# Third attention of an eight-block kernel: expert rows added, and statistics of x taken, in other tiles of the batch loop

## The chip, the cores and the metric

The kernel runs on one core of one Trainium2 chip. The metric is the device time of one execution in microseconds (us). The engines are TensorE (PE, with its weight loads as PEld), VectorE (DVE), ScalarE (ACT), GpSimd (POOL) and SyncE (SP, which issues transfers here).

## The reference

A residual stream x of 8 batches by 512 tokens by 256 features goes through four pairs of a cross attention and a feed-forward block. Each block is applied to the layer norm of x and added to x:

```
x = x + L0_xcond(layernorm(x), ctx, ...);  x = x + L0_ffn(layernorm(x))   # mixture of 8 experts, 2 per token
x = x + L1_xcond(layernorm(x), ctx, ...);  x = x + L1_ffn(layernorm(x))
x = x + L2_xcond(ctx, layernorm(x), ...);  x = x + L2_ffn(layernorm(x))   # mixture of 8 experts, 2 per token
x = x + L3_xcond(layernorm(x), ctx, ...);  x = x + L3_ffn(layernorm(x))   # ternary weights
```

The change touches only L3_xcond, the third attention of the kind with 16 heads of 16 features and 64 keys, and the end of L2_ffn which the kernel does inside it:

```
mixed = sum over the 2 chosen experts j of weight_j * expert_output_j     # end of L2_ffn
q, k, v = layernorm(x) @ Wq.T + bq, ctx @ Wk.T + bk, ctx @ Wv.T + bv
scores = (q . k per head * tau + delta) / sqrt(16)
x = x + softmax(scores) v @ Wo.T + bo
```

## The kernel before

x stays in SBUF as 32 tiles of 128 tokens, four tiles (t = 0 to 3) to each of the 8 batches (b). Each engine has its own program, written out by hand in order; semaphores tie the programs together. An engine executes its instructions in that order, so what stands behind a waiting instruction waits too.

The mixture before the attention leaves two rows for each token in DRAM (`rows_out`), one per chosen expert. `Arrival` brings them into x, batch by batch:

- SP fetches both sets of a batch's rows (`fetch`, L296) into one of two pairs of buffers. It first waits until the rows of the batch two before have all been added.
- ACT multiplies a tile of first rows by its weight (`scale_first`, L312), POOL adds it to x (`add_first`, L318), and DVE multiplies and adds the second row in one instruction (`add_second`, L325). Batches 0 and 1 are added by DVE alone ahead of the loop (`add`, L304).
- DVE takes `bn_stats` of each tile of the batch (L245) and seven small instructions of moments (L255 to L263); POOL takes the root by `pow` (L269) and the product for the shift (L272); ACT then normalises the four tiles (L649).

In the attention, step b of every engine's loop works on batch b and prepares batches b + 1 and b + 2. For a tile, DVE subtracts the maximum from the scores of the *next* tile (`softmax`, L786 and L789). PE computes scores (L537, L542), transposes the result (L598), for which ACT's exp (L685) is the drain, and multiplies by the values after every second tile (L557). ACT gives the reciprocal of the sums as exp(-ln) (L668, L670), DVE multiplies by it (L796), PE projects (L569), and DVE adds the projection to x and takes its statistics for the next block (`residual`, L813). For batch b + 1, PE turns the normalised tiles (`turn`, L506) behind the scores of tile 0 and tile 1, ACT drains them (L655), and PE computes the queries (L512). The scores banks are single: PE's scores of one tile wait for DVE's softmax of the tile before.

In step b, before the change, the work for batch b + 2 lies like this. ACT scales first rows in tiles 0 and 1, and POOL adds them. DVE adds second rows in tiles 1 and 2, and takes statistics and moments in tile 3, ahead of the keys (L764) and the residual. POOL takes the root, then the root of the output norm of batch b - 1 (whose moments DVE took in tile 2), then adds the bias of the output to batch b + 1 (L455). ACT normalises batch b + 2 at the end of tile 3. For the next block, DVE also sums (L2317) or clips (L2338, L2341) a weight matrix in tile 1 of batches 1 to 6.

Of the kernel before, what the change touches and what calls it, by code (L numbers as in the profile page):

```python
# [24 lines left out]
NB, SEQ, D = 8, 512, 256  # L25
TPB = SEQ // P
# [321 lines left out]
def attention(nc, k, L):  # L348
# [14 lines left out]
    with ctx:  # L363
# [42 lines left out]
        late_ps, late_copied = sem(nm + "late_ps"), sem(nm + "late_copied")  # L406
        out_norm = Norm(k, sem, nm + "out", k.shift if router else None)
        ternary = k.ternary if L == 3 else None
        if ternary:
# [10 lines left out]
        with nc.Block() as block:  # L420
# [20 lines left out]
            def _(pool):  # L441
# [10 lines left out]
                def add_bias(b):  # L452
                    pool.wait_ge(z_done, b + 1)
                    xs = k.x[:, b * (TPB * D):(b + 1) * (TPB * D)].rearrange("p (t d) -> p t d", t=TPB)
                    pool.tensor_tensor(xs, xs, bo[:, None, :].to_broadcast([P, TPB, D]), ALU.add).then_inc(xb_done, 1)  # L455
# [8 lines left out]
                pool.wait_ge(k.att_in, 16 * k.att_loads)  # L464
                add_bias(0)
                for b in range(NB):
                    if arrival:
                        for t in range(TPB):
                            if b + 2 < NB:
                                arrival.add_first(pool, (b + 2) * TPB + t)  # L470
                    if normed:
# [8 lines left out]
                    if in_norm and b + 2 < NB:  # L480
                        in_norm.root(pool, b + 2)
                    if b > 0:
                        out_norm.root(pool, b - 1)
                    if not normed and b + 1 < NB:
                        add_bias(b + 1)
# [5 lines left out]
                if router:  # L491
                    for r in range(NB - 3, AHEAD):
                        router.add_post(pool, r)
                out_norm.root(pool, NB - 1)

# [147 lines left out]
            def _(act):  # L643
# [28 lines left out]
                def step(b, s):  # L672
                    more = b + 1 < NB
                    for t in range(TPB):
# [17 lines left out]
                        if t == 1 and more:  # L692
                            drain_queries(b + 1, 1 - s, 0)
                        if arrival and b + 2 < NB and t < 2:
                            for i in range(2):
                                arrival.scale_first(act, (b + 2) * TPB + 2 * t + i)
                        if normed and b + 2 < NB and t == 1:
# [29 lines left out]
                if normed:  # L727
                    for j in range(TOPK):
                        normed.scale(act, j, 2)
                    normalise(1)  # L730
                for b in range(NB):
                    step(b, b % 2)
# [15 lines left out]
            def _(dve):  # L748
# [54 lines left out]
                def take_logits(r):  # L803
                    dve.wait_ge(router.lg_ps, r + 1)
                    dve.tensor_copy(router.taken(r), pr_b[:, D:LG]).then_inc(router.lg_read, 1)
# [29 lines left out]
                def step(b, s):  # L835
                    more = b + 1 < NB
                    for t in range(TPB):
# [11 lines left out]
                        if t == 3 and b + 2 < NB:  # L849
                            if coming:  # L850
                                coming.statistics(dve, b + 2)
                            drain_keys(b + 2, s)
# [6 lines left out]
                        if t == 3 or b > 0:  # L859
                            residual(n - 3)  # L860
                        if arrival and b + 2 < NB and t in (1, 2):
                            for i in range(2):
                                arrival.add_second(dve, (b + 2) * TPB + 2 * t - 2 + i)
                        if loading and b + 2 < NB and t == 1:
                            statistics(b + 2)
                        if t == 2 and b > 0:
                            out_norm.moments(dve, b - 1)
                        if ternary and t == 1:
# [49 lines left out]
                if router:  # L918
                    take_logits(NB - 4)
                scale(2 * NB - 1, 1)  # L920
                for t in range(1, TPB):
# [1869 lines left out]
```

## Time and the profile before

| | before |
|---|---|
| median of 3 runs | 2207.6 us |
| lowest and highest | 2204.77 and 2208.28 us |
| profiled execution | 2205.27 us |
| its span | 2203.5 us |
| busy PE, PEld | 1939.0 us (88%), 1445.1 us (66%) |
| busy DVE | 1310.2 us (59%) |
| busy ACT | 946.0 us (43%) |
| busy POOL | 591.1 us (27%) |
| mean granted clock of TensorE | 0.936 |

The profiled execution is one run with the hardware profiler; its span runs from the first to the last instruction, and its own time is that of the same execution as the runs are measured. The third attention lies between about 1825 and 2044 us. In the rows below a name such as L325 is a line of the kernel, `a <- b` in a timeline says which tile an instruction writes and reads, and a bracket says how long its engine sat idle before it and for what it waited. In the rows of windows stand, in this order, the stretch and its length, the busy time (and count of instructions) of PE, PEld, DVE, ACT and POOL, the granted clock of TensorE as a share of 2.4 GHz, the busy share of the DMA engines, and GB/s.

### The profile page before, as it was taken

Reading aid. Unit: us, or ns where it says so; the run is one execution under the profiler, and the core shown is the slowest. Engines: PE = TensorE matmul, PEld = TensorE weight load, DVE = VectorE, ACT = ScalarE, POOL = GpSimd, SP = SyncE. Lnnn points to the kernel's source line nnn. Section 1 sums busy time; section 2 is a strip of 40 time slices with the busy share of each in tenths; the row PEclk is TensorE's granted clock in tenths of the full one; section 3 lists DMA queues with packets and bytes.
Section 4 is the critical chain, followed back from the end, with each engine's and each line's share of the span. In section 5 each row is a group of like instructions: output and inputs, shape, how many; then the busy total and the mean of one; then the engine's idle time right before and its main releaser. Section 6 shows DMA issues by size and latency. Waiting matters only on the chain. (4 is left out here: it accounts for less than half of the span.)

```text
span 2203.5 us, 37784 instructions
## 1 busy us (share of the span) xinstructions
PE 1939.0 (88%) x11932; PEld 1445.1 (66%) x11933; DVE 1310.2 (59%) x3008; ACT 946.0 (43%) x2132; POOL 591.1 (27%) x598
## 2 busy tenths in 40 slices
PE   6999589999758887999979759999999995999787
PEld 3677346666535554666667549999999993666455
DVE  5877846666468887787745452222222215999786
ACT  2554334444346543333314333333333333455787
POOL 1122446666434421011000032222222221232000
PEclk8999589999979998999989669999999997999999
DMA  7000221111151104000001321111111114100001
GB/s 279 11 21 29 81 67 62 62 62 62 48 168 58 58 1 167 0 1 0 0 10 49 150 99 36 35 38 34 37 37 35 38 32 146 59 20 1 10 29 39
DMA packets 71268, 119.69 MB, mean 54 GB/s; under 512 B 13664, under 2 KB 54880, under 8 KB 68096
## 3 DMA queue, kind: packets, MB, share of 16 engines
q1 hardware_dynamic: 55904, 78.89, 10.3%
q0 software_dynamic: 13680, 37.37, 5.3%
q10 hardware_dynamic: 1584, 2.13, 0.3%
q8 instruction: 59, 0.97, 0.2%
q14 instruction: 41, 0.34, 0.0%
HBM read 87.03 MB, written 31.33 MB: 54 GB/s over the span
## 5 line engine op out<-in xcount | busy, mean ns | idle before, releaser
L1488 ACT ACTIVATE e_hT<-psum,x_bt 128x128 f32<-128x128 f32 x568 | 154.2, 383 | 340.8 <-PE psum L1451 336.1
L269 POOL TENSOR_TENSOR rstd<-lnt,half 128x4 f32<-128x4 f32 (+1 forms) x72 | 73.2, 1016 | 766.4 <-DVE lnt L263 766.4
L1451 PEld LDWEIGHTS psum<-e_xT,e_w 128*128 128x128 f32 x2272 | 266.2, 193 | 7.2 <-ACT e_xT L1481 3.6
L1451 PE MATMUL psum<-e_xT,e_w 128*128 128x128 f32 x2272 | 266.8, 276 | 3.0 <-ACT e_xT L1481 3.0
L1460 PE MATMUL psum<-m_w,e_hT 128*128 x1136 | 256.8, 379 | 0.0
L1460 PEld LDWEIGHTS psum<-m_w,e_hT 128*128 128x128 f32 x1136 | 210.4, 190 | 25.7
L1510 DVE COPY e_w<-m_w 128x2048 f32 x71 | 87.1, 1227 | 231.2 <-PE psum L1451 226.8
L1307 ACT ACTIVATE e_hT<-psum,x_bt,x_gt 128x128 f32<-128x128 f32 x284 | 106.7, 456 | 142.8 <-PE psum L1274 142.8
L786 DVE TENSOR_REDUCE a_mx<-psum 128x8 f32<-128x512 f32 x192 | 123.2, 683 | 66.3 <-PE psum L542 65.8
L1392 POOL DMA_INDIRECT rows_out<-e_y,dst x106 | 105.6, 997 | 206.2 <-DVE e_y L1520 175.2
L1384 POOL DMA_INDIRECT e_x<-rows_in,src x142 | 141.9, 999 | 56.7 <-issue 35.3
L685 ACT ACTIVATE a_pT<-psum 128x512 f32<-128x512 f32 x192 | 104.0, 592 | 111.4 <-PE psum L598 111.4
L1284 PE MATMUL psum<-m_w,e_hT 128*128 x568 | 140.6, 390 | 4.0 <-ACT e_hT L1307 3.6
L1265 PE MATMUL psum<-m_w,e_xT 128*128 x284 | 139.7, 615 | 1.3 <-ACT e_xT L1299 1.2
L1981 PE MATMUL psum<-f_w,f_q 128*128 128x256 f32 x512 | 121.4, 382 | 14.7 <-DVE f_q L1868 14.7
L1981 PEld LDWEIGHTS psum<-f_w,f_q 128*128 128x128 f32 x512 | 96.9, 191 | 54.7 <-issue 30.5
L1968 PE MATMUL psum<-f_zT,f_w 128*128 128x512 f32 x256 | 122.7, 606 | 0.8 <-DVE f_q L1865 0.8
L789 DVE TENSOR_TENSOR a_pr<-psum,a_mx 128x512 f32<-128x512 f32 x192 | 123.0, 682 | 0.6
L1284 PEld LDWEIGHTS psum<-m_w,e_hT 128*128 128x128 f32 x568 | 102.5, 190 | 21.1 <-issue 5.5
L569 PE MATMUL psum<-att_wo,a_oT 128*128 128x256 f32 x384 | 101.4, 388 | 10.4 <-DVE x_res L813 8.4
L512 PE MATMUL psum<-a_zT,att_wq 128*128 128x512 f32 x192 | 101.4, 654 | 7.7 <-ACT a_qT L662 5.6
L598 PE MATMUL psum<-cst,a_pr 128*128 128x128 f32 x768 | 106.2, 283 | 0.2
(308 smaller groups left out, 3562.2 us busy)
## 6 DMA issues: line engine op xcount, KB each, us to landing
m_w<-in_L_ffn_w SPq DMA_DIRECT2D x16, 1024.0 KB, 12.6
m_w<-in_L_ffn_w SPq DMA_DIRECT2D x16, 512.0 KB, 12.1
m_w<-rows_out SPq DMA_DIRECT2D x16, 512.0 KB, 5.9
a_ar_g<-rows_out SPq DMA_DIRECT2D x16, 512.0 KB, 5.1
rows_in<-a_r_z SPq DMA_DIRECT2D x14, 512.0 KB, 2.9
x_res<-in_x SPq DMA_DIRECT2D x8, 512.0 KB, 7.0
m_w<-rows_in SPq DMA_DIRECT2D x8, 512.0 KB, 3.9
out_x<-x_res SPq DMA_DIRECT2D x8, 512.0 KB, 3.0
```

Source lines behind the costliest of these rows:

```text
L598: mm = pe.transpose(tr_b[g][:, i, :], pr[t % 2][:, at:at + P], k.ident)
L786: dve.tensor_reduce(mx[g][:, :], wide[g], AX.X, ALU.max).then_inc(s_max, 1)
L789: dve.tensor_tensor(pr[t % 2][:, g * W:(g + 1) * W].rearrange("p (h l) -> p h l", h=HPC), wide[g], mx[g][:, :, None].to_broadcast([P, HPC, ...
L1265: mm = pe.matmul(h_b[s][:, c * 512:(c + 1) * 512], xT[s][:, kk, :], w1[:, bass.ds(e * (DC * F) + (kk * F + c * 512), 512)], start=(kk == 0 ...
L1284: mm = pe.matmul(y_b[:, 0:D], hT[s][:, f, :], w2[:, bass.ds(e * (FC * D) + f * D, D)], start=(f == 0), stop=(f == FC - 1))
L1307: g = act.activation(hT[s][:, f, :], hT_b[:, f, :], ACT.Gelu, bias=bt[:, col], scale=gt[:, col] if norm else 1.0)
L1384: pool.indirect_dma_start(out=xin[j % 2][:, :], out_offset=None, in_=k.zs[:, :], in_offset=bass.IndirectOffsetOnAxis(ap=k.src[:, j:j + 1], ...
L1451: mm = pe.matmul(h_b[s][:, f, :], w1[:, kk, f * P:(f + 1) * P], xT[s][:, kk, :], start=(kk == 0), stop=(kk == DC - 1))
L1460: mm = pe.matmul(y_b[s][:, 0:D], hT[s][:, f, :], k.w2[:, bass.ds(e * (FC * D) + f * D, D)], start=(f == 0), stop=(f == FC - 1))
L1488: g = act.activation(hT[s][:, f, :], h_b[s][:, f, :], ACT.Gelu, bias=bt[:, bass.ds(e * FC + f, 1)])
L1968: mm = pe.matmul(hb[f % HS][:, :], w1[:, kk, f * P:(f + 1) * P], zT[s][:, kk, :], start=(kk == 0), stop=(kk == DC - 1))
L1981: mm = pe.matmul(yb[t % 2][:, 0:D], q[s][:, g, t * P:(t + 1) * P], w2[:, g, :], start=(g == 0), stop=(g == FC - 1))
```

## The change

All of it holds only where `arrival` is set, in the third attention.

- ACT scales first rows of batch b + 3, not b + 2, in tiles 1 and 2, not 0 and 1, of step b. Those of batch 2 are scaled ahead of the loop.
- POOL adds them a batch further ahead too: batch 2 before the loop; in step b two tiles of batch b + 3 before the root for x, two behind the roots. The bias add of batch b + 1 moves from the end of POOL's step to its head.
- DVE adds all four second rows of batch b + 2 in tile 0, behind the residual, and takes the statistics and moments of x in tile 2, not 3.
- The moments of the output norm come two batches late (`lag` = 2), in tile 1, and those of batch 6 behind the loop, before the last multiply by the reciprocal. POOL takes its roots with the same lag, and two behind the loop.

```diff
--- before.py
+++ after.py
@@ -405,6 +405,7 @@
         router = RouterFront(k, sb, sem, nm + "r_", L, 2) if L == 0 else None
         late_ps, late_copied = sem(nm + "late_ps"), sem(nm + "late_copied")
         out_norm = Norm(k, sem, nm + "out", k.shift if router else None)
+        lag = 2 if arrival else 1
         ternary = k.ternary if L == 3 else None
         if ternary:
             ternary.signals(sem, nm + "f3_")
@@ -463,11 +464,16 @@
                     normed.sum(pool, 2)
                 pool.wait_ge(k.att_in, 16 * k.att_loads)
                 add_bias(0)
+                if arrival:
+                    for t in range(TPB):
+                        arrival.add_first(pool, 2 * TPB + t)
                 for b in range(NB):
                     if arrival:
-                        for t in range(TPB):
-                            if b + 2 < NB:
-                                arrival.add_first(pool, (b + 2) * TPB + t)
+                        if b + 1 < NB:
+                            add_bias(b + 1)
+                        if b + 3 < NB:
+                            for t in range(2):
+                                arrival.add_first(pool, (b + 3) * TPB + t)
                     if normed:
                         if b + 2 < NB:
                             normed.u_norm.root(pool, b + 2)
@@ -479,9 +485,12 @@
                             normed.sum(pool, b + 3)
                     if in_norm and b + 2 < NB:
                         in_norm.root(pool, b + 2)
-                    if b > 0:
-                        out_norm.root(pool, b - 1)
-                    if not normed and b + 1 < NB:
+                    if b >= lag:
+                        out_norm.root(pool, b - lag)
+                    if arrival and b + 3 < NB:
+                        for t in range(2, TPB):
+                            arrival.add_first(pool, (b + 3) * TPB + t)
+                    if not coming and b + 1 < NB:
                         add_bias(b + 1)
                     if router:
                         if b == 0:
@@ -491,7 +500,8 @@
                 if router:
                     for r in range(NB - 3, AHEAD):
                         router.add_post(pool, r)
-                out_norm.root(pool, NB - 1)
+                for b in range(NB - lag, NB):
+                    out_norm.root(pool, b)
 
             @block.tensor
             def _(pe):
@@ -691,9 +701,9 @@
                                 drain_turn(b + 1, 0)
                         if t == 1 and more:
                             drain_queries(b + 1, 1 - s, 0)
-                        if arrival and b + 2 < NB and t < 2:
+                        if arrival and b + 3 < NB and t in (1, 2):
                             for i in range(2):
-                                arrival.scale_first(act, (b + 2) * TPB + 2 * t + i)
+                                arrival.scale_first(act, (b + 3) * TPB + 2 * t - 2 + i)
                         if normed and b + 2 < NB and t == 1:
                             normed.normalise_sum(act, b + 2)
                         if normed and b + 3 < NB and t in (0, 2):
@@ -728,6 +738,9 @@
                     for j in range(TOPK):
                         normed.scale(act, j, 2)
                     normalise(1)
+                if arrival:
+                    for t in range(TPB):
+                        arrival.scale_first(act, 2 * TPB + t)
                 for b in range(NB):
                     step(b, b % 2)
                 reciprocals(2 * NB - 1)
@@ -847,8 +860,8 @@
                         if t == 2:
                             scale(2 * b, 0)
                         if t == 3 and b + 2 < NB:
-                            if coming:
-                                coming.statistics(dve, b + 2)
+                            if normed:
+                                normed.statistics(dve, b + 2)
                             drain_keys(b + 2, s)
                         if normed and t == 0 and b + 2 < NB:
                             normed.sum_statistics(dve, b + 2)
@@ -858,13 +871,15 @@
                             dve.wait_ge(xb_done, b + 1)
                         if t == 3 or b > 0:
                             residual(n - 3)
-                        if arrival and b + 2 < NB and t in (1, 2):
-                            for i in range(2):
-                                arrival.add_second(dve, (b + 2) * TPB + 2 * t - 2 + i)
+                        if arrival and b + 2 < NB and t == 0:
+                            for i in range(TPB):
+                                arrival.add_second(dve, (b + 2) * TPB + i)
+                        if arrival and b + 2 < NB and t == 2:
+                            arrival.statistics(dve, b + 2)
                         if loading and b + 2 < NB and t == 1:
                             statistics(b + 2)
-                        if t == 2 and b > 0:
-                            out_norm.moments(dve, b - 1)
+                        if t == 3 - lag and b >= lag:
+                            out_norm.moments(dve, b - lag)
                         if ternary and t == 1:
                             for i in (0, 1):
                                 if 0 < b < 4:
@@ -917,6 +932,8 @@
                     step(b, b % 2)
                 if router:
                     take_logits(NB - 4)
+                if lag > 1:
+                    out_norm.moments(dve, NB - 2)
                 scale(2 * NB - 1, 1)
                 for t in range(1, TPB):
                     residual(NT - TPB + t, last_b[t - 1])
```

## Rows read from the trace of the kernel before

**Rows 1.** Windows of four rounds of the third attention; columns in its second line.

```profile
core 0: us, PE busy (x) PEld busy (x) DVE busy (x) ACT busy (x) POOL busy (x), PEclk, DMA share, GB/s
1861.49:1882.60 21.11, 20.52 (x176) 13.38 (x176) 16.34 (x39) 11.02 (x22) 6.34 (x7) 1.00 0.15 52
1882.60:1906.60 24.00, 22.36 (x184) 14.77 (x184) 22.14 (x54) 12.73 (x26) 7.32 (x8) 1.00 0.15 44
...
1978.74:2002.75 24.01, 22.36 (x184) 14.76 (x184) 22.62 (x55) 14.69 (x28) 8.89 (x8) 1.00 0.00 1
2002.75:2023.76 21.01, 20.08 (x164) 12.96 (x164) 18.66 (x40) 11.85 (x21) 3.36 (x2) 1.00 0.01 2
```

**Rows 2.** Waits, 1820 to 2050 us: total, times, longest us.

```profile
ACT a_z L649 <- POOL a_shift L272: 37.0, 8, 12.2
```

**Rows 3.** Timeline of DVE: start us, us, instruction, [idle before it].

```profile
1883.50 0.69 DVE L796 TENSOR_TENSOR a_oT<-psum,a_rec 128x512 f32<-128x512 f32 x1 [0.91 <-ACT a_rec L670]
...
1894.86 0.42 DVE L813 TENSOR_TENSOR x_res<-psum,x_res 128x256 f32<-128x256 f32 x1 [0.57 <-PE psum L569]
...
1895.66 0.86 DVE L325 SCALAR_TENSOR_TENSOR x_res<-a_ar_g,wt,x_res 128x256 f32<-128x256 f32 x2
1896.44 0.16 DVE L255 TENSOR_TENSOR lnt<-stats 128x4 f32<-128x4 f32 x1
...
1897.21 1.28 DVE L786 TENSOR_REDUCE a_mx<-psum 128x8 f32<-128x512 f32 x2
...
1899.61 1.39 DVE L245 BATCH_NORM_STATS2 stats<-x_res 128x6 f32<-128x256 f32 x4
...
1901.81 0.87 DVE L764 SCALAR_TENSOR_TENSOR a_kb<-psum,att_bk,cst 128x256 f32<-128x256 f32 x2
```

**Rows 4.** Timeline of POOL, the root for x.

```profile
1901.98 1.01 POOL L269 TENSOR_TENSOR rstd<-lnt,half 128x4 f32<-128x4 f32 x1 [11.15 <-DVE lnt L263]
```

**Rows 5.** Timeline of ACT.

```profile
1859.48 1.09 ACT L685 ACTIVATE a_pT<-psum 128x512 f32<-128x512 f32 x2 [5.76 <-PE psum L598]
...
1898.25 1.09 ACT L685 ACTIVATE a_pT<-psum 128x512 f32<-128x512 f32 x2 [3.38 <-PE psum L598]
1903.30 2.07 ACT L649 ACTIVATE a_z<-x_res,a_shift,rstd 128x256 f32<-128x256 f32 x4 [3.96 <-POOL a_shift L272]
...
1906.84 0.63 ACT L670 ACTIVATE a_rec<-a_rec 128x512 f32<-128x512 f32 x1
```

**Rows 6.** Timeline of PE.

```profile
1882.65 0.39 PE L537 MATMUL psum<-a_dl,ones 64*128 64x512 bf16 x2 [0.58 <-DVE a_pr L789]
...
1902.50 1.09 PE L598 MATMUL psum<-cst,a_pr 128*128 128x128 f32 x8
...
1905.42 0.66 PE L506 MATMUL psum<-cst,a_z 128*128 128x128 f32 x4 [0.96 <-ACT a_z L649]
...
1906.66 0.39 PE L537 MATMUL psum<-a_dl,ones 64*128 64x512 bf16 x2 [0.58 <-DVE a_pr L789]
```

**Rows 7.** Timeline of DVE in other rounds.

```profile
1869.16 1.29 DVE L786 TENSOR_REDUCE a_mx<-psum 128x8 f32<-128x512 f32 x2 [3.04 <-PE psum L542]
...
1986.32 1.63 DVE L2341 TENSOR_SCALAR f_rawu<-f_rawu 128x2048 f32<-128x2048 f32 x1
...
2011.36 1.29 DVE L786 TENSOR_REDUCE a_mx<-psum 128x8 f32<-128x512 f32 x2 [0.59 <-PE psum L542]
...
2037.92 0.69 DVE L796 TENSOR_TENSOR a_oT<-psum,a_rec 128x512 f32<-128x512 f32 x1 [0.44 <-ACT a_rec L670]
```

**Rows 8.** The tile of expert rows: count, duration ns least/median/most, first and last start.

```profile
L312 ACT ACTIVATE a_ar_g<-a_ar_g,wt x24: 493/497/518, 1860.9 to 1985.4; 128x256 f32<-128x256 f32 x24
L318 POOL TENSOR_TENSOR x_res<-x_res,a_ar_g x24: 723/732/1704, 1861.5 to 1986.8; 128x256 f32<-128x256 f32 x24
...
DMA to landing us min/median/max: 3.9/5.1/10.6
```

**Rows 9.** Window behind the attention, columns as in rows 1.

```profile
2044.00:2053.50 9.50, 7.08 (x20) 3.02 (x20) 4.36 (x10) 3.77 (x4) 0.00 (x0) 0.50 0.00 1
```

## The prediction

> **What bounds the kernel now.** The page's busy shares say little here, since the edit touches only the third attention, so I read first the windows of its batches. I call a *round* the stretch from one batch's softmax of tile 1 to the next one's. Seven rounds run from 1861.5 to 2023.8 us; the five in the middle (batches 1 to 5) take 24.0 us each, and in all of them TensorE stands at its full clock [rows 1]. In a middle round PE is busy 22.36 us and DVE 22.14: neither is idle for long, and the reader is to look for which of them closes the loop, not for one bottleneck.
>
> The waits come next. ACT waits 37.0 us in eight pieces for POOL's shift before it normalises [rows 2]. In time it reads so: DVE ends the softmax of the next batch's tile 0, takes the four statistics of x (1899.61) and its moments, POOL takes its root (1901.98), ACT normalises from 1903.30 [rows 3 to 5]. ACT is in order, so exp of the new batch's tile 0 stands behind that, and its reciprocal (1906.84) is 0.91 us too late for DVE's multiply by it; the same wait is at 1883.50 [rows 3, 5]. PE waits 0.96 us for z and then 0.58 us for DVE's softmax (1906.66) [rows 6].
>
> The visible z wait is not the loop. Even with z early, PE would stand at 1906.66, since DVE's softmax ends only then. I follow the loop back from there. DVE is without a pause from 1894.86 to that end, and at 1894.86 it had waited 0.57 us for PE's projection of tile 2 [rows 3]. PE, from its scores at 1882.65 to that projection, has no wait that matters [rows 6]: this is 12.2 us of PE, then 11.8 us of DVE, sum 24.0. That is the loop that sets the round.
>
> **The change, part by part.** Only L == 3 is touched; the other attentions keep their order.
>
> *Second adds.* DVE's two pairs of second adds leave tiles 1 and 2 (a pair takes 0.78 us from start to start, 1895.66 to 1896.44 [rows 3]) and all four stand in tile 0: 1.56 us there. Their rows must be landed, scaled and first-added, which the next part gives.
>
> *Statistics of x.* They take 1901.81 − 1899.61 = 2.20 us and leave tile 3 for tile 2. *Output moments* (1897.21 − 1896.44 = 0.77 us) leave tile 2 for tile 1, two batches late instead of one.
>
> So DVE does no instruction more or less in a round. On the 11.8 us stretch behind the projection, the pair and the moments go away (0.78 + 0.77 = 1.55 us), while the statistics stay on it. The PE–DVE loop falls to 24.01 − 1.55 = 22.46 us. The engines have floors of their own: DVE 24.01 − 0.91 − 0.57 = 22.53 us, PE 24.01 − 0.96 − 0.58 = 22.47 us. All three lie within 0.1 us, so the floor is DVE's work and little of a further gain is possible.
>
> *What becomes late next.* The shift is ready about 1.5 us after the statistics (1901.81 to 1903.30 [rows 3, 5]), now about 17 us into the round, when ACT ends exp of tile 3 (1898.25 + 1.09, 16.7 us into it): the stall of four us there is gone. Exp of tile 0 then waits for PE's transposes, which come 19.85 us after the round's start (1882.65 to 1902.50 [rows 6]). With 0.7 us to exp's start, as at tile 3, 1.1 us for exp and twice about 0.6 us for the reciprocal's Ln and Exp (0.63 [rows 5]), the reciprocal stands at about 22.85 us. DVE wants it at the round's end, 22.53. If the round is 22.53 + w and w is 22.85 less the round, w = 0.16: the round takes about 22.7 us, 1.3 less. This holds for batches 1, 2 and 3: 3 × 1.3 = 3.9 us.
>
> In batches 4 and 5 the weight clipping (1986.32 and its partner before it [rows 7]) stands in for the shorter weight sums, and there was no wait for the projection. DVE's floor is 24.01 − 0.91 = 23.10 us; I take 0.85 each for small waits of PE on the later softmax of tile 3: 1.7 us.
>
> In the first round PE is busy 20.52 of 21.11 us and in the last 20.08 of 21.01 [rows 1]. DVE waits for PE there (3.04 us at 1869.16, 0.59 at 2011.36 [rows 7]), so what DVE saves is mostly lost. Bounds 0 and 0.9 us each (the reciprocal wait that goes, as in rows 3); I take 0.2 each, since PE's idle time is all that there is: 0.4 us.
>
> *The tail.* The moments of batch 6 move behind the weight scales and before the last multiply, which waited 0.44 us (2037.92 [rows 7]). 0.77 − 0.44 gives 0.3 us lost; bounds 0 and 0.8. The extra root on POOL (1.01 us) is hidden by DVE's last three residual adds.
>
> *First adds.* ACT scales batch 2's four rows and POOL adds them ahead of the loop: four by 0.50 us and four by 0.73 us [rows 8]. ACT sat idle 5.76 us before the first exp (1859.48 [rows 5]), and POOL's adds end some 2 us before that on the same reckoning. Without that cover it would cost about 2.2 us. In the loop the same work is a batch earlier, in tiles 1 and 2 of ACT, which idled 3.4 us before exp of tile 3 [rows 5]. On POOL the root for x stands behind two first adds, which wait for ACT in tile 1 of the same batch, some 8 us before the statistics: free. Then come the roots (to about 17.9 us: 15.6 + 1.3 + 1.0 [rows 4]), two adds (1.5) and, from about 19.4 to 21.8 us, the bias add of 2.35; DVE's second adds start at about 24.1. Slack 2.3 us.
>
> *Transfers.* No DMA is added. SP's fetch of batch b+3 waits for the second adds of batch b+1, which now come in tile 0 of batch b−1 and so earlier; a pair lands in 5.1 us, the slowest in 10.6 [rows 8], over 20 us before its use.
>
> Here a rule bears on it: the Trainium skill, SBUF — State Buffer, section "SBUF: two separate sides", says that GpSimd and certain VectorE instructions take a shared pair of ports in turn, the loser blocked for a whole instruction. The rows show such a case: the usual POOL add takes 0.73 us and one 1.70 us [rows 8], at the time of DVE's clipping (1986.32 [rows 7]). By the rule the four adds of tile 0, which read two tiles in SBUF, must not meet POOL's bias add of 2.35 us; by the order above they don't, and the sum stays. It returns as the third rival.
>
> **Sum.** 3.9 + 1.7 + 0.4 − 0.3 = 5.7 us. The profiled execution took 2205.27 us (span 2203.5): 2199.6 by its own time. The median of the three runs is 2207.6, 2.3 us above it; measured against that median I predict 2207.6 − 5.7 = 2201.9 us. About 0.2%, or 4.4 us, is what a measurement of this kernel can tell from no change.
>
> **The rivals.**
>
> 1. *PE takes the wait* (0.27). The four adds in tile 0 push the softmaxes of tiles 2 and 3 later: 0.78 and, with the moments, 1.55 us before tile 3's. My reckoning ends tile 3's softmax 11.8 us into the round where PE wants it at 12.1. For it: the margin is 0.3 us, and one more wait of DVE in tile 0 or 1 eats it. Then PE, with a floor of 22.47, is pushed out by each further microsecond. Against: DVE waits for nothing there but the reciprocal. With 0.7 us more per round the five rounds give 5.7 − 3.5 = 2.2 us: 2205.4 us, no change to be measured.
>
> 2. *More than the sum* (0.08). PE's turn of z was also a little late, and the first and last rounds could give their 0.9 us each: 5.7 + 1.4, and 0.3 for the tail: 7.4 us, 2200.2 us.
>
> 3. *POOL comes late and takes the second adds with it* (0.05). This one is slower. DVE's four adds now stand at the head of the round and wait for POOL's two last first adds, which stand behind two roots; the bias add follows. If POOL ran more than 2.3 us later than I put it, DVE would wait or be blocked for up to the bias add's 2.35 us in five rounds: 11.8 − 5.7 = 6.1 us lost, 2213.7 us. Against: before, POOL idles 11.15 us ahead of the root [rows 4].
>
> The share left is the forecast's, 0.60. One thing outside can shift any of them: after the attention TensorE stands at half clock (1.2 GHz) for 9.5 us, with 7.08 us of PE work [rows 9]. The attention's end moves by 6 us; if the clock fell or rose at another moment, up to 3.5 us (half of 7.08) is won or, with a stretch that much longer, lost. The Trainium skill, TensorE: Matmul & The Clock Gate, section "Part 1: The HAM clock gate", says that the array's clock follows recent activity by windows that run free of the kernel; by that a shift of either sign is as likely. From the rows alone I can't tell the sign either, so I take nothing, and let the range hold half of it.
>
> **How the numbers follow.** The forecast alone spans 2200 to 2204 us. The range reaches rival 1 and the half of the clock term above it, and rival 2 less 1 us below: 2199.0 to 2206.5; rival 3 is left out. Faster by over 0.2% is most of the forecast (0.52 of 0.60) and rival 2: 0.60. Slower is rival 3 with a little of the clock: 0.06. Within 0.2% is the rest, 0.34.
>
> **What would show it.** Rounds of 22.7 us in batches 1 to 3 and 23.1 in 4 and 5; ACT's wait before its normalising down from 4 us to under 1; DVE's wait for the reciprocal down from 0.9 to about 0.2; PE's 0.96 us wait for z gone; and the last multiply 0.3 us late. If the rounds take 23.4 us or more and PE waits for DVE before the scores of the next tile 0, rival 1 holds. If DVE waits for POOL at the four adds, rival 3 does. A round that stays at 24.0 would mean that I followed the wrong loop.

## The result, and the profile after

The changed kernel took 2198.73 us in the median of seven runs, the kernel before, beside it, 2205.17 us in seven. The ratio is 0.9974 with a 95% interval of 0.9965 to 0.9983: about 5.7 us less (3.7 to 7.7), where the prediction had 5.7 us less. The two medians lie 6.4 us apart. The predicted 2201.9 us was counted from 2207.6, the median of the three runs known then; counted from 2205.17 the same sum gives 2199.5. In its profiled execution the span is 2196.9 us against 2203.5.

The agreement is in part luck, as the rounds show. The table gives the time from PE's scores of tile 2 in one batch (L537 before, L547 after) to those in the next, read from the timeline of PE; the tail runs from the last of these to the first transpose of the next stage. The stage runs from the first POOL instruction of the attention to that transpose.

| us | round 0 | 1 | 2 | 3 | 4 | 5 | 6 | tail | stage |
|---|---|---|---|---|---|---|---|---|---|
| before | 21.09 | 24.01 | 24.01 | 24.01 | 24.12 | 24.01 | 21.00 | 20.81 | 219.36 |
| after | 20.86 | 22.45 | 23.62 | 23.62 | 24.01 | 22.71 | 20.70 | 21.03 | 215.41 |
| predicted, middle rounds | | 22.7 | 22.7 | 22.7 | 23.15 | 23.15 | | | |

The stage gained 4.0 us, not 5.7. The other 2.7 us of the difference between the two spans lie ahead of it: the stage starts at 1825.3 us before and at 1822.6 us after, with the same instructions ahead of it. Behind it nothing moved: from the first instruction of ACT in the next stage to the end are 158.9 us in both.

Most of those 2.7 us stand at the very start of the program, in the first attention, which the change doesn't touch. The same eight matmuls and the same four instructions of ACT, before and after:

```profile
32.10 1.91 PE L542 MATMUL psum<-a_kb,a_qT 64*128 64x256 f32 x8
56.72 2.07 ACT L649 ACTIVATE a_z<-x_res,a_shift,rstd 128x256 f32<-128x256 f32 x4
```

```profile
32.02 1.03 PE L552 MATMUL psum<-a_kb,a_qT 64*128 64x256 f32 x8
54.47 2.07 ACT L659 ACTIVATE a_z<-x_res,a_shift,rstd 128x256 f32<-128x256 f32 x4
```

The two programs are level at the matmuls, but between 31 and 40 us the granted clock of TensorE is 0.50 before and 1.00 after, and at the normalising the kernel before is 2.25 us behind. The clock rose earlier in this execution of the changed kernel. That isn't the change's doing: the same eight matmuls are slow in seven of the experiments below, all variants of the changed kernel, and fast in experiment 7, a variant of the kernel before.

The windows of rounds 1, 2, 4 and 5 of the changed kernel, with the columns of [rows 1]:

```profile
1879.87:1902.32 22.45, 22.07 (x185) 14.88 (x186) 21.34 (x47) 12.92 (x26) 6.36 (x7) 1.00 0.15 47
1902.32:1925.94 23.62, 22.15 (x186) 14.93 (x187) 22.98 (x54) 13.01 (x27) 7.30 (x8) 1.00 0.14 46
1949.56:1973.57 24.01, 22.15 (x186) 14.94 (x187) 23.38 (x56) 12.97 (x27) 7.33 (x8) 1.00 0.01 1
1973.57:1996.28 22.71, 22.14 (x184) 14.93 (x185) 22.12 (x54) 13.29 (x25) 4.53 (x4) 1.00 0.00 1
```

DVE is busy 22.98 us in round 2, where it was 22.14 before (as in round 1 [rows 1]), although it has the same instructions to do. The timeline of DVE in rounds 0 to 2 shows where:

```profile
1880.07 0.69 DVE L809 TENSOR_TENSOR a_oT<-psum,a_rec 128x512 f32<-128x512 f32 x1 [0.25 <-ACT a_rec L680]
...
1903.91 1.66 DVE L325 SCALAR_TENSOR_TENSOR x_res<-a_ar_g,wt,x_res 128x256 f32<-128x256 f32 x4
...
1908.67 0.15 DVE L255 TENSOR_TENSOR lnt<-stats 128x4 f32<-128x4 f32 x1
1908.74 0.16 DVE L256 TENSOR_TENSOR lnt<-stats 128x4 f32<-128x4 f32 x1
1908.81 0.16 DVE L257 TENSOR_TENSOR mean<-stats 128x4 f32<-128x4 f32 x1
1909.01 0.64 DVE L259 SCALAR_TENSOR_TENSOR lnt<-lnt 128x4 f32<-128x4 f32 x1
1909.58 0.15 DVE L260 TENSOR_SCALAR mean<-mean 128x4 f32<-128x4 f32 x1
1909.64 0.70 DVE L261 TENSOR_SCALAR lnt<-lnt 128x4 f32<-128x4 f32 x1
1910.38 0.16 DVE L263 TENSOR_TENSOR lnt<-lnt 128x4 f32<-128x4 f32 x1
1910.46 2.34 DVE L2334 TENSOR_REDUCE f_wsum<-f_rawu 128x1 f32<-128x1024 f32 x2
```

The wait for the reciprocal is 0.25 us (1880.07; it was 0.91 [rows 3]) and the four second adds stand in a row from 1903.91. But then the moments of the output norm, seven instructions on 128x4 elements, take from 1908.67 to 1910.46, 1.79 us instead of 0.77 [rows 3]. Two of them, L259 and L261, take 0.64 and 0.70 us; the usual time is 0.16. I call an instruction *held* when it takes longer than its usual time beside one of the other engine. POOL in the same time:

```profile
1908.90 1.41 POOL L318 TENSOR_TENSOR x_res<-x_res,a_ar_g 128x256 f32<-128x256 f32 x2 [7.99 <-ACT a_ar_g L312]
1918.86 1.01 POOL L269 TENSOR_TENSOR rstd<-lnt,half 128x4 f32<-128x4 f32 x1 [8.54 <-DVE lnt L263]
```

It adds two tiles of first rows from 1908.90 to 1910.31. The four second adds take 1.66 us and DVE waits for nothing ahead of them, so rival 3 (POOL late) did not come. ACT's normalising and what PE waits for:

```profile
1896.40 2.08 ACT L659 ACTIVATE a_z<-x_res,a_shift,rstd 128x256 f32<-128x256 f32 x4
...
1920.18 2.08 ACT L659 ACTIVATE a_z<-x_res,a_shift,rstd 128x256 f32<-128x256 f32 x4 [0.26 <-POOL a_shift L272]
```

```profile
1901.35 0.60 PE L516 MATMUL psum<-cst,a_z 128*128 128x128 f32 x4
1902.32 0.39 PE L547 MATMUL psum<-a_dl,ones 64*128 64x512 bf16 x2 [0.37 <-DVE a_pr L802]
...
1915.33 0.39 PE L547 MATMUL psum<-a_dl,ones 64*128 64x512 bf16 x2 [1.02 <-DVE a_pr L802]
```

ACT waited 3.96 us for the shift [rows 5] and now none in round 1 and 0.26 us in round 2. PE's turn of z (1901.35) has no wait any more, and the wait behind it is 0.37 us. At 1915.33 stands a new one: 1.02 us for DVE's softmax of tile 3. The end of the stage on DVE:

```profile
2027.97 0.42 DVE L826 TENSOR_TENSOR x_res<-psum,x_res 128x256 f32<-128x256 f32 x1 [0.90 <-PE psum L579]
...
2031.31 0.69 DVE L809 TENSOR_TENSOR a_oT<-psum,a_rec 128x512 f32<-128x512 f32 x1
```

### The profile page after: what moved, and what is told of

The parts are those of the page before. It is cut to its first block and busy times, and to the rows that moved or that the text cites. A ratio compares the mean times of both kernels' runs of the same rounds, so it can differ in the third digit from the quotient of the medians.

```text
span 2196.9 us, 37769 instructions
## 1 busy us (share of the span) xinstructions
PE 1932.8 (88%) x11917; PEld 1444.1 (66%) x11933; DVE 1311.0 (60%) x3008; ACT 946.9 (43%) x2132; POOL 589.0 (27%) x598
```

## The experiments

All are variants of the changed kernel except the seventh, which starts from the kernel before. Each ratio is to the kernel before on the same chip, with its 95% interval. The median in each case, and the rounds from each profile:

| kernel | median us | ratio | 1 | 2 | 3 | 4 | 5 | tail | stage |
|---|---|---|---|---|---|---|---|---|---|
| 1 moments behind sums | 2198.11 | 0.9973 (0.9964 to 0.9982) | 22.45 | 22.59 | 22.50 | 23.95 | 22.70 | 21.03 | 213.15 |
| 2 moments in tile 0 | 2197.25 | 0.9968 (0.9957 to 0.9980) | 22.44 | 22.60 | 22.56 | 23.50 | 22.72 | 21.11 | 212.85 |
| 3 no lag | 2198.00 | 0.9972 (0.9963 to 0.9981) | 23.05 | 23.05 | 23.04 | 23.12 | 23.05 | 20.80 | 214.23 |
| 4 statistics in tile 3 | 2202.78 | 0.9999 (0.9990 to 1.0008) | 22.84 | 24.26 | 24.26 | 24.49 | 23.58 | 21.03 | 218.85 |
| 5 first adds behind roots | 2196.99 | 0.9966 (0.9954 to 0.9979) | 22.45 | 22.60 | 22.59 | 22.97 | 22.72 | 21.12 | 212.42 |
| 6 and the tail | 2198.86 | 0.9970 (0.9959 to 0.9981) | 22.45 | 22.59 | 22.59 | 22.98 | 22.72 | 20.89 | 212.19 |
| 7 lag alone | 2204.34 | 0.9997 (0.9987 to 1.0007) | 23.25 | 23.69 | 23.68 | 24.79 | 24.46 | 21.03 | 219.36 |
| 8 adds alone | 2200.44 | 0.9986 (0.9977 to 0.9994) | 23.39 | 23.38 | 23.39 | 24.29 | 23.59 | 20.81 | 217.42 |
| 9 POOL's side | 2196.33 | 0.9959 (0.9945 to 0.9972) | 22.44 | 22.60 | 22.51 | 22.99 | 22.72 | 21.03 | 212.40 |
| 10 four adds in tile 1 | 2205.46 | 1.0007 (0.9998 to 1.0016) | 22.45 | 24.12 | 24.10 | 28.11 | 22.80 | 21.04 | 220.72 |
| 11 changed, again | 2199.68 | 0.9976 (0.9965 to 0.9986) | 22.45 | 23.61 | 23.62 | 24.01 | 22.72 | 21.05 | 215.51 |
| 12 the sixth, again | 2197.61 | 0.9972 (0.9960 to 0.9984) | 22.44 | 22.60 | 22.59 | 22.97 | 22.73 | 20.89 | 212.33 |

In the two kernels that were profiled twice (11 and 12 against their first runs) the rounds repeat to 0.02 us and the stage to 0.14, so they decide; the whole time can only confirm.

**1. The moments behind the weight sums.**

```diff
-                        if t == 3 - lag and b >= lag:
-                            out_norm.moments(dve, b - lag)
                         if ternary and t == 1:
...
                                     ternary.clip_weights(dve, 2 * (b - 4) + i)
+                        if t == 3 - lag and b >= lag:
+                            out_norm.moments(dve, b - lag)
```

> The changed kernel, with the output moments of a batch put behind the weight sums (or clips) of tile 1 instead of ahead of them; same tile, same instructions. Theory: in rounds 2 to 4 the seven small moments take 1.8 us instead of 0.77 because two of them are held (0.64 and 0.70 us instead of 0.16) while POOL adds two tiles of first rows; behind the sums POOL is done, so the moments take 0.8 us again, PE's wait of 1.02 us before its scores goes, rounds 2 and 3 fall from 23.6 to about 22.7 us and round 4 from 24.0 to about 23.1: some 2.7 us less than the changed kernel. Rival: DVE has simply too much work between tile 1 and tile 3's softmax since the four second adds came into tile 0; then the order inside tile 1 changes nothing and the rounds stay at 23.6, 23.6 and 24.0.

The timeline of DVE in round 2, behind the sums:

```profile
1913.74 2.33 DVE L2334 TENSOR_REDUCE f_wsum<-f_rawu 128x1 f32<-128x1024 f32 x2
...
1916.33 0.16 DVE L259 SCALAR_TENSOR_TENSOR lnt<-lnt 128x4 f32<-128x4 f32 x1
1916.41 0.16 DVE L260 TENSOR_SCALAR mean<-mean 128x4 f32<-128x4 f32 x1
1916.48 0.16 DVE L261 TENSOR_SCALAR lnt<-lnt 128x4 f32<-128x4 f32 x1
```

L259 and L261 take 0.16 us here, and rounds 2 and 3 are 22.59 and 22.50 us, though DVE does the same work in the same tile. The rival falls. Round 4 stayed at 23.95 us, against the expected 23.1: there the clipping stands ahead of the moments. POOL's adds and it meet: the second clipping instruction took 1.64 us instead of 1.23, and POOL's pair 3.50 us, so that it still ran when the moments came and held the first of them (L255, 0.68 us).

**2. The moments in tile 0.**

```diff
+                        if t == (0 if arrival else 2) and b >= lag:
+                            out_norm.moments(dve, b - lag)
                         if arrival and b + 2 < NB and t == 0:
                             for i in range(TPB):
                                 arrival.add_second(dve, (b + 2) * TPB + i)
...
-                        if t == 3 - lag and b >= lag:
-                            out_norm.moments(dve, b - lag)
```

> The changed kernel, with the output moments in tile 0, ahead of the four second adds, instead of tile 1. POOL is idle there (it waits 8 us for ACT). Theory (moments held by POOL's adds): as in the kernel with the moments behind the sums, rounds 2 and 3 at about 22.7 us, round 4 at 23.1 us. Rival (too much DVE work ahead of tile 3's softmax): it is as much work as before there, so 23.6, 23.6 and 24.0 us.

Round 4 on DVE, first the moments and then the clipping (L2355), which now meets POOL's adds in their place:

```profile
1954.83 0.16 DVE L259 SCALAR_TENSOR_TENSOR lnt<-lnt 128x4 f32<-128x4 f32 x1
...
1954.98 0.16 DVE L261 TENSOR_SCALAR lnt<-lnt 128x4 f32<-128x4 f32 x1
...
1960.03 1.78 DVE L2355 TENSOR_SCALAR f_rawg<-f_rawg,f_wscale 128x2048 f32<-128x2048 f32 x1
```

Rounds 2 and 3 came out as expected. Round 4 took 23.50 us, 0.4 more than expected: one clipping instruction took 1.78 us where it takes 1.28 without company.

**3. No lag.**

```diff
-        lag = 2 if arrival else 1
+        lag = 1
```

> The changed kernel with lag = 1: output moments one batch late, in tile 2 behind the statistics of x; none behind the loop. Theory: no moments meet POOL's adds, but they are back on the stretch of DVE behind PE's projection: 24.0 - 0.78 = 23.2 us in all of rounds 1 to 5 (116 us together, as the changed kernel's 116.4), the tail 0.2 us shorter. Rival (the tile in which the moments stand doesn't matter, only that they aren't held): 22.7 us in rounds 2 and 3.

All five rounds are 23.05 to 23.12 us: the expected 23.2 less 0.15, and nowhere the rival's 22.7. So the seven moments cost about 0.45 us of their 0.77 on the stretch behind the projection even when nothing holds them (22.60 us in experiment 2), and this kernel, without the lag, has a stage 1.2 us shorter than the changed one.

**4. The statistics back in tile 3.**

```diff
                         if t == 3 and b + 2 < NB:
-                            if normed:
-                                normed.statistics(dve, b + 2)
+                            if coming:
+                                coming.statistics(dve, b + 2)
                             drain_keys(b + 2, s)
...
-                        if arrival and b + 2 < NB and t == 2:
-                            arrival.statistics(dve, b + 2)
```

> The changed kernel with the statistics of x back in tile 3; the rest as changed. Theory: ACT waits for the shift again and DVE 0.9 us or more for the reciprocal in every round; with DVE as the engine that sets the round this adds about 0.7 us to each: round 1 at about 23, rounds 2 and 3 at about 24.3, round 4 at 24.8, round 5 at 23.4 us; some 3 us more than the changed kernel. Rival (the move of the statistics is worth nothing by itself, the gain is the shorter stretch behind the projection): the rounds as in the changed kernel, 22.45, 23.6, 23.6, 24.0, 22.7 us.

ACT's wait for the shift in round 2, and PE's wait for the softmax of tile 3:

```profile
1925.60 2.08 ACT L659 ACTIVATE a_z<-x_res,a_shift,rstd 128x256 f32<-128x256 f32 x4 [2.78 <-POOL a_shift L272]
```

```profile
1918.23 0.39 PE L547 MATMUL psum<-a_dl,ones 64*128 64x512 bf16 x2 [1.36 <-DVE a_pr L802]
```

ACT waits 2.78 us again and DVE 0.91 us for the reciprocal, and rounds 1 to 5 are 0.4 to 0.9 us longer than in the changed kernel, 3.0 us together: near the expected values, and against the rival. Without this part of the change the rest is worth 0.5 us of stage, and no difference can be measured (0.9999).

**5. All first adds behind the roots,** with the moments in tile 0 as in experiment 2.

```diff
-                        if b + 3 < NB:
-                            for t in range(2):
-                                arrival.add_first(pool, (b + 3) * TPB + t)
...
                     if arrival and b + 3 < NB:
-                        for t in range(2, TPB):
+                        for t in range(TPB):
                             arrival.add_first(pool, (b + 3) * TPB + t)
```

> The kernel with the output moments in tile 0, and POOL's two first adds of tile 1 put behind the roots with the other two. In round 4 of the kernel with the moments in tile 0 one clipping of weights took 1.78 us instead of 1.28 while POOL added. Theory: with no POOL instruction beside it the clipping takes 1.28 us, round 4 falls from 23.50 to about 23.0 us, the other rounds stay (22.4, 22.6, 22.6, 22.7 in rounds 1, 2, 3, 5). POOL's queue gets 1.4 us longer behind the roots, with its bias add ending about 1 us before DVE's second adds. Rival (POOL comes late): DVE waits for POOL at the second adds, or is held by the bias add, and rounds 1 to 4 grow by up to 1 us.

Round 4 falls from 23.50 to 22.97 us and the others stay. POOL didn't come late: in round 2 its bias add ends at 1925.98 us, and DVE's second adds start at 1928.00 without a wait.

**6. And the tail.** The edits of experiments 2 and 5, and:

```diff
+                        if lag > 1 and n == NT - 2:
+                            out_norm.moments(dve, NB - 2)
...
-                if lag > 1:
-                    out_norm.moments(dve, NB - 2)
                 scale(2 * NB - 1, 1)
```

> As the kernel with all first adds behind the roots, and the output moments of batch 6 in tile 2 of the last batch instead of ahead of the last multiply. DVE waits 0.90 us for PE there in the changed kernel, so they should cost nothing, and the last multiply stands where the reciprocal lets it: tail 20.8 us instead of 21.1. Stage from its first POOL instruction to the next stage's first transpose about 212.2 us, against 219.4 of the kernel before and 215.4 of the changed one. Rival: PE's wait for that batch's residual eats it, as before (0.36 us), tail 21.1.

The last multiply on DVE:

```profile
2034.30 0.69 DVE L806 TENSOR_TENSOR a_oT<-psum,a_rec 128x512 f32<-128x512 f32 x1 [0.45 <-ACT a_rec L677]
```

It waits 0.45 us for the reciprocal, as before [rows 7], so the moments are off that path. The tail is 20.89 us, 0.23 less than in experiment 5 and 0.08 more than before. The stage, at 212.2 us, is the shortest of all. In whole runs that 0.2 us can't be seen.

**7. The lag alone,** on the kernel before.

```diff
+        lag = 2 if arrival else 1
...
-                        if t == 2 and b > 0:
-                            out_norm.moments(dve, b - 1)
+                        if t == 3 - lag and b >= lag:
+                            out_norm.moments(dve, b - lag)
```

(with POOL's roots and the moments behind the loop as in the changed kernel)

> The kernel before, with the output moments two batches late in tile 1 as the only edit. Theory: DVE's stretch behind the projection is 0.77 us shorter (loop 23.24 us), but the reciprocal's wait of 0.91 us stays, and DVE's floor with it is 23.44 us: round 1 about 23.2, rounds 2 and 3 about 23.4 us if POOL's adds (which come later in tile 1 here) miss the moments, up to 24.4 if they meet; rounds 4 and 5 at 24.0 or up to 1 us more. Rival (the reciprocal's wait sets the round by itself): 24.0 us everywhere.

DVE and POOL in round 2:

```profile
1903.47 0.69 DVE L798 TENSOR_TENSOR a_oT<-psum,a_rec 128x512 f32<-128x512 f32 x1 [0.90 <-ACT a_rec L672]
...
1909.52 0.60 DVE L263 TENSOR_TENSOR lnt<-lnt 128x4 f32<-128x4 f32 x1
```

```profile
1909.38 1.42 POOL L318 TENSOR_TENSOR x_res<-x_res,a_ar_g 128x256 f32<-128x256 f32 x2 [3.56 <-ACT a_ar_g L312]
```

The wait for the reciprocal is as it was, but rounds 1 to 3 are below 24.0 us, so the rival falls. Here only the last of the seven moments meets POOL's add (from 1909.38) and takes 0.60 us: rounds 2 and 3 are 23.69 us, 0.25 above the expected 23.44. In round 4 (24.79 us) two of the moments, L259 and L261, take 0.69 and 0.70 us from 1956.81, beside POOL's pair from 1956.76; in round 5 (24.46 us) L263 takes 0.61 us and the first clipping instruction 1.83 instead of 1.28, beside the pair from 1981.55. The lag puts the moments where POOL adds already in the kernel before. The sum over the stage is nothing: 219.36 us as before, ratio 0.9997.

**8. The adds alone:** experiment 4 with lag = 1.

> The changed kernel with lag = 1 and the statistics of x back in tile 3, so that only the first rows a batch ahead and the second adds in tile 0 are left of the change. Theory: the stretch behind the projection is 0.78 us shorter (loop 23.23 us), and DVE's floor with the reciprocal's wait is 23.44 us: rounds 1 to 3 at 23.3 to 23.5, rounds 4 and 5 at 24.0; some 1.8 us less than the kernel before. Rival (the second adds in tile 0 push tile 3's softmax out by as much as they free behind it): rounds at 24.0.

DVE's wait for the reciprocal:

```profile
1927.65 0.69 DVE L809 TENSOR_TENSOR a_oT<-psum,a_rec 128x512 f32<-128x512 f32 x1 [0.91 <-ACT a_rec L680]
```

Rounds 1 to 3 are 23.39 us, by DVE's floor with that wait (23.44), as expected. Rounds 4 and 5 (24.29 and 23.59) are on either side of the expected 24.0: POOL's adds meet the clipping in round 4 (1.63 us instead of 1.23), and in round 5 there are none. Against experiment 3, which has the statistics in tile 2 and is otherwise the same, the statistics in tile 3 cost 0.34 us in each of rounds 1 to 3.

**9. POOL's side.** The diff of experiment 5, on the changed kernel as it is; DVE's program untouched.

> The changed kernel, with POOL's two first adds of tile 1 put behind the roots; DVE's program is untouched, its moments stay in tile 1. Theory (the moments are held by POOL's adds): they take 0.8 us again, rounds 2 and 3 at 22.6 us and round 4 at 23.0 us, stage about 212.5 us. Rival (it is their place on DVE that counts, between the residual and the sums): they stay at 1.8 us, rounds 23.6, 23.6, 24.0.

The same two moments on DVE, in tile 1 as in the changed kernel:

```profile
1911.49 0.16 DVE L259 SCALAR_TENSOR_TENSOR lnt<-lnt 128x4 f32<-128x4 f32 x1
...
1911.64 0.16 DVE L261 TENSOR_SCALAR lnt<-lnt 128x4 f32<-128x4 f32 x1
```

They take 0.16 us. Rounds 2, 3 and 4 are 22.60, 22.51 and 22.99 us. With experiment 1 this takes the meeting apart from both sides: moving either partner, and nothing else, restores the time.

**10. Four first adds in tile 1.**

```diff
-                        if arrival and b + 3 < NB and t in (1, 2):
-                            for i in range(2):
-                                arrival.scale_first(act, (b + 3) * TPB + 2 * t - 2 + i)
+                        if arrival and b + 3 < NB and t == 1:
+                            for i in range(TPB):
+                                arrival.scale_first(act, (b + 3) * TPB + i)
```

(and POOL's four adds all ahead of the root)

> The changed kernel, with all four first adds of a batch in tile 1 (ACT scales all four there), ahead of the root, so that POOL adds 2.8 us there instead of 1.4. Theory: a small moment instruction that meets a POOL add waits for its end, and in turn the next ones do for the next add: the moments, 1.8 us with two adds, take up to 1.2 us more with four, and rounds 2 and 3 go to 24.2 to 24.8 us, round 4 to 24.5 or more. Rival (they are held once whatever POOL does behind): rounds as in the changed kernel, 23.6, 23.6, 24.0; ACT's 0.9 us more in tile 1 is covered by its idle time.

DVE and POOL in round 2:

```profile
1907.58 0.65 DVE L259 SCALAR_TENSOR_TENSOR lnt<-lnt 128x4 f32<-128x4 f32 x1
...
1908.23 0.70 DVE L261 TENSOR_SCALAR lnt<-lnt 128x4 f32<-128x4 f32 x1
1908.96 0.65 DVE L263 TENSOR_TENSOR lnt<-lnt 128x4 f32<-128x4 f32 x1
```

```profile
1907.48 2.80 POOL L318 TENSOR_TENSOR x_res<-x_res,a_ar_g 128x256 f32<-128x256 f32 x4 [7.99 <-ACT a_ar_g L312]
```

Three of the seven are held instead of two: rounds 2 and 3 grew by 0.5 us to 24.1, just below the theory's 24.2 and clear of the rival. In round 4, where POOL's adds start a little earlier against the moments, four are held. Round 4 grew by 4.1 us, far more than either side reckoned with. PE's wait for tile 3's softmax, and windows behind it, which show the granted clock:

```profile
1963.54 0.39 PE L544 MATMUL psum<-a_dl,ones 64*128 64x512 bf16 x2 [2.43 <-DVE a_pr L799]
```

```profile
1964.00:1965.00 1.00, 1.00 (x10) 0.66 (x6) 0.97 (x3) 0.00 (x0) 0.00 (x0) 0.89 0.00 0
1965.00:1971.00 6.00, 6.00 (x28) 4.99 (x28) 5.06 (x17) 1.92 (x4) 2.17 (x3) 0.50 0.01 3
1971.00:1972.00 1.00, 1.00 (x13) 0.44 (x16) 0.52 (x2) 1.00 (x3) 0.00 (x0) 0.70 0.00 0
```

PE idled 2.43 us, worked for some 1.2 us at the full clock, and then TensorE stood at its lower level, 1.2 GHz, for some 6.8 us (by the shares 0.89, 0.50 and 0.70 of the three windows). The work there runs at about half speed (eight transposes take 1.97 us where they take 1.09). PE is busy all that time, so about half of it, 3.4 us, is lost by this estimate, and PE's wait is 1.0 us longer than in the changed kernel; together they account for about the 4.1 us.

**11. The changed kernel again.**

> The changed kernel unchanged, beside the others on the same chip. Its stage takes 215.4 us against 219.4 before, 4.0 us less, while its measured time was 6.4 us below that of before. Theory: rounds again 22.45, 23.6, 23.6, 24.0, 22.7 us, ratio about 0.998, since nothing outside the stage differs. Rival: the change helps outside the stage as well, ratio 0.9974 or below.

The rounds are the same to 0.02 us, the stage 215.5 us. The ratio is 0.9976 (0.9965 to 0.9986). By the stage alone (4.0 of 2205 us) it would be 0.9982, which lies inside this interval and that of the first measurement. The rival's 0.9974 does too, so that this run doesn't tell them apart.

**12. The sixth kernel again.**

> The kernel with the moments in tile 0, all first adds behind the roots and batch 6's moments in tile 2 of the last batch, unchanged from its first run. Its stage takes 212.2 us, 3.2 us less than the changed kernel's and 7.2 us less than before: ratio to before 0.9967 and to the changed kernel 0.9985. Rival: what the stage gains is lost in the stages around it (the half clock behind the attention), ratio to before as the changed kernel's.

Its ratio to before is 0.9972 (0.9960 to 0.9984) and its median 2.1 us below the changed kernel's beside it (ratio of the medians 0.9991). The stage says 3.2 us. That the sixth kernel is faster than the changed one is shown by the stage, and only suggested by the whole times. The best of all measured is the ninth (0.9959), whose stage is 0.2 us longer; the intervals of the two overlap, so the whole times don't tell them apart.

## Why the prediction was right, and where it was not

*The bound and the loop: right.* PE and DVE set the round together. Taking 0.78 us off the stretch behind the projection (experiment 8) gave 0.6 us, and both parts of 1.55 us, with the statistics moved, gave 22.45 to 22.6 us where nothing held DVE: the predicted floor of 22.5. The statistics in tile 2 are needed for it, since the reciprocal's wait fell from 0.91 to 0.25 us only then (experiments 4, 7 and 8 keep it).

*Rounds 2 and 3: the term that failed.* The step read "DVE does no instruction more or less in a round", and took its seven moments at 0.77 us. They took 1.79 us, since POOL's first adds met them in tile 1, where the lag had moved them (experiment 7 meets the adds of the kernel before too). The predicted 22.7 became 23.62 us in rounds 2 and 3, and 24.01 instead of 23.15 in round 4: 0.9 us each, 2.7 us in all. Experiments 1, 2 and 9, each moving only one of the partners, bring rounds 2 and 3 back to 22.5 to 22.6. The rule of the Trainium skill, SBUF — State Buffer, "SBUF: two separate sides", was weighed against the wrong pair of instructions: I weighed the four second adds against the bias add and left the small moments out, though L259 takes two inputs from SBUF as well. The traces agree with the rule as to L259: 0.64 us beside POOL's adds and 0.16 without.

*Rival 1* came true in rounds 2 to 4 by the prediction's own sign: 23.4 us or more, and PE waits for DVE before the scores of the next tile 0 (1.02 us, in round 4 1.41). Its warning, that one more wait of DVE in tile 0 or 1 eats the margin, is what happened. The work moved ahead isn't enough for it: in experiment 2 the four adds and the moments stand there as well, and PE has no such wait. The margin of 0.3 us that the prediction reckoned wasn't there: a hold of 1.02 us cost PE 1.02 us. The rival had it in all five rounds at 0.7 us each; it came in three, and its 2205.4 us did not come.

*Round 1* was sized wrong the other way: 22.45 us, not 22.7. With the lag the loop has no output moments in batch 1, 0.77 us less work, which I had overlooked. *Round 5*: 22.71 us, not 23.15. I had taken the clipping from 1986.32 [rows 7], where POOL's add ran beside it (1.63 us); alone it takes 1.23. The kernel before shows that meeting in rounds 4 and 5, not once as the prediction read it from the longest add of [rows 8]; POOL's pairs there took 3.24 and, in round 5, 2.98 us:

```profile
1985.56 2.98 POOL L318 TENSOR_TENSOR x_res<-x_res,a_ar_g 128x256 f32<-128x256 f32 x2 [3.56 <-ACT a_ar_g L312]
```

In the changed kernel POOL adds nothing in round 5, since the rows come a batch earlier.

*The ends.* Round 0 gained 0.23 and round 6 0.30 us (0.2 each predicted), the tail lost 0.22 (0.3 predicted). The clock behind the attention brought nothing: 158.9 us from there to the end, before and after.

*The sum.* The stage's terms are 1.56 + 0.39 + 0.39 + 0.11 + 1.30 in the rounds, 0.53 in rounds 0 and 6, less 0.22 in the tail: 4.1 us, of which the stage shows 4.0. The prediction's 5.7 was 1.7 too large. The measured 5.7 lies right on it, but its interval (3.7 to 7.7) holds the stage's 4.0 too; that the whole time hit it is luck. The range has a slip of its own: by its rule it should run from 2199.2 (2200.2 less 1) to about 2207.2 us (2205.4 and half of 3.5), not from 2199.0 to 2206.5.

*The start of the stage.* Over the fourteen profiles the stage starts anywhere from 1821.0 to 1828.8 us, with the same instructions ahead of it: that is what moves whole times by several us, since from the stage's end to the last instruction are 158.3 to 158.9 us in all. The early matmuls part the profiles in two. In six, the eight near 32 us take 1.03 us and the stage starts by 1823.4; in eight they take 1.91 to 1.92 us, the time at the lower clock, and it starts at 1824.3 or later. Part of the rest is PE's first matmul, which waits for its data until 11.2 to 13.0 us. What sets the moment of the clock's rise stays open; no run was made for it.

## What to carry to other kernels

When two engines set a loop together, follow the chain that goes from one to the other and back, and take out what lies on it; the wait that looks largest need not be on it (here PE's for z), or only through another (ACT's 4 us for the shift count by the 0.91 us that DVE then waits for the reciprocal). When a change moves work in time, look at what runs *beside* it in its new place on the other engine, down to instructions of 0.16 us, before taking its old duration; a DVE instruction may be several times longer next to a POOL one. And where the gain is a few tenths of a per cent, measure it by the stage's own periods, which repeated to 0.02 us here, not by the whole time, which wanders by more than the gain, and look for the wandering ahead of the change.

## What the runs showed of the hardware

- DVE instructions on 128x4 elements, 0.16 us each, took 0.50 to 0.73 us beside POOL's adds of 0.7 us each: one or two of seven were held with two adds, three or four with four. Which ones depends on the moment: L255, L257, L259, L261 and L263 were all held in one run or another. L261, a tensor_scalar with one tensor input, was held as well as L259, which has two. L260, of the same kind and shape, was not: it stood right behind a held one.
- Not every DVE instruction was held. In the changed kernel the softmax of a tile, which reads PSUM, took its usual 1.29 us at 1923.27 and one `bn_stats` its usual 0.43 us at 1922.32, beside POOL's adds (until 1922.5) and its bias add of 2.37 us (from 1922.45).
- The hold goes both ways: the clipping of weights took 1.78 instead of 1.28 us beside POOL's adds (experiment 2), and POOL's two adds 3.50 us instead of 1.42 beside the clipping (experiment 1).
- A wait of PE of 2.43 us inside a busy loop was followed by some 6.8 us at the lower clock (experiment 10, round 4). In experiment 4 PE's longest wait in these rounds was 1.57 us, in the changed kernel 1.41, and the granted clock stayed at 1.00 in both. Why the clock fell in the one and not in the others wasn't tried.
- The clock at the program's start rose early in six of fourteen profiles and late in eight, though the instructions are the same; at 55 us into the program the kernel before was 2.25 us behind the changed one for it.
